# Attention and mixture of experts on one core: GpSimd's row transfers tied to TensorE's results

## The reference, cut to what matters

```python
h = layernorm(x)
q, k_new, v_new = h @ wq.T, h @ wk.T, h @ wv.T
k, v = concat([ctx, k_new]), concat([ctx, v_new])      # 64 cached rows + 64 new ones
x = x + softmax(q @ k.T / 16) @ v @ wo.T
h = layernorm(x)
probs = softmax(h @ router.T)                          # 32 experts
topv, topi = top_k(probs, 4); topv = topv / sum(topv)
out = sum over the 4 of topv * ((silu(h @ w_gate[e]) * (h @ w_up[e])) @ w_down[e])   # inner width 96
out += sigmoid(h @ sgate_w) * ((silu(h @ sw_gate) * (h @ sw_up)) @ sw_down)          # inner width 512
x = x + out
```

## Time and profile before

| what | value |
|---|---|
| median of the timed runs | 516.37 us |
| recorded span of the profiled execution | 667.5 us |
| recorded span less the median | 151.1 us |
| TensorE busy (matmuls, share of the recorded span) | 574.4 us, 86% |
| VectorE busy | 363.5 us, 54% |
| ScalarE busy | 288.7 us, 43% |
| GpSimd busy | 269.4 us, 40% |
| mean granted TensorE clock | 0.903 |

### The profile page before, as it was taken

How to read it: one execution, slowest core, us unless ns; L and a number is a source line. 1 busy time by engine, 2 the same in 40 slices (tenths; PEclk the granted TensorE clock), 3 DMA queues, 4 the chain that set the end, 5 groups by cost and what they waited for, 6 DMA issues and landing times. The chain is left out here.

```text
span 667.5 us, 13365 instructions
## 1 busy us (share of the span) xinstructions
PE 574.4 (86%) x3945; PEld 478.3 (72%) x3945; DVE 363.5 (54%) x1199; ACT 288.7 (43%) x719; POOL 269.4 (40%) x344
## 2 busy tenths in 40 slices
PE   8998787788887777899998988778877898979998
PEld 7997777677777565677886666656666676658886
DVE  5575455555555351565553635445454444536998
ACT  5775444555444440613463545444454544401111
POOL 1004444445555458380034544445454454560000
PEclk9999788987778788699997977988989978989999
DMA  5573544444433322293145444544444544228996
GB/s 160 181 227 128 170 156 129 144 134 145 138 123 113 110 76 107 70 244 98 31 130 148 131 140 124 140 136 139 130 140 140 150 131 132 87 86 330 368 340 230
DMA packets 65956, 100.77 MB, mean 151 GB/s; under 512 B 9856, under 2 KB 52864, under 8 KB 65792
## 3 DMA queue, kind: packets, MB, share of 16 engines
q1 hardware_dynamic: 48704, 60.30, 30.6%
q0 software_dynamic: 12672, 35.41, 14.7%
q10 hardware_dynamic: 4512, 4.23, 1.9%
HBM read 55.92 MB, written 43.97 MB: 150 GB/s over the span
## 5 line engine op out<-in xcount | busy, mean ns | idle before, releaser
L512 POOL DMA_INDIRECT returned<-arena,back x136 | 130.6, 960 | 171.7 <-DVE back L1629 81.5
L481 POOL DMA_INDIRECT sent<-rows,slot x128 | 129.9, 1015 | 159.2 <-issue 82.7
L1100 PE MATMUL bank<-w_gu,arena 128*128 x416 | 94.7, 363 | 26.6 <-issue 16.6
L1100 PEld LDWEIGHTS bank<-w_gu,arena 128*128 128x128 f32 x416 | 73.0, 205 | 32.8 <-issue 32.8
L1580 DVE TENSOR_TENSOR arena<-bank,arena 128x192 f32<-128x192 f32 x68 | 24.2, 356 | 113.5 <-ACT arena L737 94.5
L737 ACT ACTIVATE arena<-bank 128x192 f32<-128x192 f32 x68 | 22.3, 329 | 127.0 <-remote 70.5
L806 PE MATMUL bank<-w_hi_all,att_split 128*128 128x256 f32 x256 | 56.8, 314 | 18.6 <-issue 18.6
L1597 DVE TENSOR_SCALAR arena<-bank,back_to 128x256 f32<-128x256 f32 x136 | 59.0, 476 | 6.3 <-remote 5.3
L806 PE MATMUL bank<-att_split,w_hi_all 128*128 128x256 f32 x256 | 55.5, 336 | 1.4 <-issue 1.3
L710 ACT COPY hnt<-w_gu 128x384 f32 x128 | 55.7, 509 | 0.0
L806 PEld LDWEIGHTS bank<-w_hi_all,att_split 128*128 128x128 f32 x256 | 42.4, 208 | 18.2 <-issue 18.2
(11 more groups left out here) (216 smaller groups left out, 1128.6 us busy)
## 6 DMA issues: line engine op xcount, KB each, us to landing
arena<-returned SPq DMA_DIRECT2D x16, 1024.0 KB, 7.2
loaded<-sent SPq DMA_DIRECT2D x104, 134.0 KB
w_gu<-w_gate_up SPq DMA_DIRECT2D x32, 192.0 KB
sent<-rows SPq DMA_DIRECT2D x4, 1072.0 KB, 6.2
loaded<-sent SPq DMA_DIRECT2D x128, 33.5 KB
resid<-x SPq DMA_DIRECT2D x16, 256.0 KB, 2.9
att_plain<-ctx_t SPq DMA_DIRECT2D x16, 256.0 KB, 3.1
out<-resid ACTq DMA_DIRECT2D x7, 512.0 KB, 4.9
```

Of the source, the lines that this page charges most:

```text
L481: pool.indirect_dma_start(out=sent, out_offset=bass.IndirectOffsetOnAxis(ap=slot[:, 2 * b + j, k:k + 1], axis=0), in_=rows[:, u, j, :], in ...
L512: pool.indirect_dma_start(out=returned, out_offset=bass.IndirectOffsetOnAxis(ap=back[:, t:t + 1], axis=0), in_=down_e[u][:, s, :], in_offs ...
L1100: last = pe.matmul(view[:, s, :], rows_t[:, s, c, :], w_gu[:, c, bass.ds(e[s - 2 + len(e)], 1), :] .rearrange("p e f -> p (e f)"), start=( ...
```

## The change

GpSimd gets two kinds of new waits; nothing else changes. In attention, for 0 < n < 16, each second turn first waits for a result of TensorE's step n: turn 0 for `c_psum` = n, turn 2 for `k_psum` = n+1, turn 4 for `xnt_psum` = n+2, turn 6 for `o_psum` = n. The waits stand only where there is something to send, so from step 5 on. In the experts, the second transfer of pair p waits until the down product of pair p+1 is done.

```diff
                 for turn in range(SENT_A_STEP):
                     if may_send(n - 6 if turn < 4 else n - 5):
+                        if turn % 2 == 0 and 0 < n < blocks:
+                            wait(pool, ("c_psum", "k_psum", "xnt_psum", "o_psum")[turn // 2],
+                                 (n, n + 1, min(n + 2, blocks), n)[turn // 2])
                         send()
                         if n > blocks:
                             breathe(1)
...
                 wait(pool, "down_ready", pair + 1)
                 for s in range(2):
                     t = 2 * pair + s
+                    if s == 1 and pair + 1 < pairs:
+                        wait(pool, "worked_psum", worked(pair + 1))
                     pool.indirect_dma_start(
```

## The result

The changed kernel takes 520.01 us in the median of 20 runs (516.77 to 523.84) against 516.03 for the kernel before; the ratio is 1.0101, 95% interval 1.0074 to 1.0128. It is slower by 1.0%, some 5 us, where no change was forecast. The time lies inside the forecast range, 511.5 to 521, but the direction was missed.

A forecast was written before the change was run, and what follows sets the result against it. TensorE alone was taken as the bound; its unstarved stages sum to 510.9 us, 5.5 below the timed median. The change's terms add 0 to 516.4 us, with +0.9 at worst; forecast 516.4 us, range 511.5 to 521.

The forecast's parts named there:

- The recorded stalls are not in the timed runs: Whole kernel: TensorE's starved stretches belong to the recording; the change can take away at most 5.5 us.
- The sum of unstarved stages: Whole kernel with TensorE never starved: 59.0, 96.0, 101.2, 182.0 and 72.7 us, together 510.9.
- the 151.1 us: Recorded span 667.5 us less timed median 516.4; nearly all of it said to belong to the recording.
- The first transfer 3.7 us later, then each mark already there: Attention: GpSimd's stream starts 3.7 us later; within a step or two the waits are met and cost nothing.
- No wait is added from step 16 on, where steps are longer and GpSimd catches up; so that end doesn't move: After attention's new waits: GpSimd catches up, so SyncE's wait for the last transfer ends as before; cost 0.
- There are over 20 us in any case: Between the end of SyncE's wait for attention transfers and first tile use: over 20 us of slack.
- If the 3.7 us were not absorbed they would be all of it: Attention: the cost is 0, hidden by slack; without that slack, the late start's 3.7 us would be the cost.
- The experts' wait costs nothing: Experts: the 67 added waits are met or nearly met, with slack of 6 us or more; cost 0.
- Rival 2: Experts: GpSimd becomes the bound through restarts after waits, giving 519.5 to 525.8 us; chance 0.13.
- The last landing moves by at most 1.3 us: End of the experts: the last landing doesn't move, at worst by 1.3 us, adding 0.9 us to the time.
- Rival 3: Attention: transfers hold back VectorE's operations, 13 us in all, 529.6 us, chance 0.03; a smaller loss, 518 to 519, 0.05.
- A recorded span of 610 to 665 us: Changed kernel's profile: span expected at 610 to 665 us, against 667.5 before, since waits bind in the recorded execution.

The follow-up runs named there:

- e1: The kernel before the change, unchanged, run and profiled again: 515.74 us, ratio 0.9999.
- e9: The kernel before, with SyncE reading the first four pairs' row numbers ahead of its wait for the attention transfers: 511.86 us, ratio 0.9957.
- e4: The kernel before with a single wait, GpSimd's very first attention transfer waiting for `xnt_psum` of step 5: 518.74 us, ratio 1.0073.
- e6: The kernel before with a single wait, the first attention transfer waiting for the next step's `xnt_psum`: 528.70 us, ratio 1.0304.
- e3: The kernel before with only the new wait in the experts, none in attention: 515.42 us, ratio 0.9989.

## Why the prediction was wrong

- *The recorded stalls are not in the timed runs*: right. The sum of unstarved stages, 510.9 us, met the span of e1, 511.5, and no part of the 151.1 us was there to be won. That the sum met it so well was luck: two terms were off and cancelled. The experts take 191.9 us, not 182.0 (even in e9, where TensorE waits for tile loads for 0.3 us only, the same instructions take 188.8 us, 5.90 a double pair and not 5.69), and the stretch before them 93.7, not 101.2. The text put the stalls down to the recording; e1 was recorded too and has none.
- *The first transfer 3.7 us later, then each mark already there*: right, 3.9 us, and GpSimd slower than TensorE's step, as the row count said.
- *"No wait is added from step 16 on, where steps are longer and GpSimd catches up; so that end doesn't move"*: this is the step that failed. GpSimd had no idle time between 54.2 and 225.2 us in which to catch up, and the end moved, by 1.4 us in the changed kernel and 4.5 in e4. The arithmetic for it stood in the text: 128 transfers at 1.35 us are 173 us, from 56 on, so until 229.
- *"There are over 20 us in any case" between that end and the first tile use*: wrong, and the root of it. The 20 us were read from the execution recorded ahead of the prediction, where TensorE was slowed and GpSimd had gaps of 5 to 10 us. The sum had been moved to the unstarved pace, and this slack had not: by the sum's own terms the first tile use would have come at 59.0 + 96.0 + 101.2 - 11.8 = 244.4 us, with the stream ending at 229. In e1 the last transfer starts at 225.2, the first load goes at 228.8, the first tile is used at 234.7, and about 3 us of lateness are absorbed there (e4, e6). Lateness within these 3 us still costs, behind the first tile, which no term of the prediction had.
- *"If the 3.7 us were not absorbed they would be all of it"*: the price was named, and e4's 3.8 us lie on it, but not by that way: the delay does not pass through one for one. In the changed kernel 1.4 of the 3.9 us reach the loads, and the time grows by 5.2. The case stood beside the rivals rather than as one, with no chance of its own.
- *The experts' wait costs nothing*: right within the noise, e3 at 0.9989. Rival 2 falls. *The last landing moves by at most 1.3 us*: the tail is as long as before, 73.2 against 73.1 us.
- *Rival 3, transfers beside other work of VectorE*: ten attention steps are 95.8 us in both windows, so no such loss is seen. The traces show the hold-up the other way round: the transfer waits for VectorE's operation, and its wait lies inside its recorded time (0.96 to 1.89 us), while the operations of L1296 and L1235 keep theirs whether they start during a transfer or not (684 to 693 and 1218 to 1224 ns in e1). Rows 8 looked at the engine that is not lengthened.
- *A recorded span of 610 to 665 us*: wrong, 516.2, for the reason above.

## What to carry to other kernels

Work out each queue's total (number of instructions times their spacing) and set it against the stretch it has: an engine that shows idle time in one execution can be the bound in another. When a sum is moved to another pace, every slack that it leans on has to be moved too, read from both ends at that pace. A wait put at the head of a stream without idle time is not made good by idle time later, however early it stands, and however quickly the waits behind it cost nothing. What it costs in the end is another question, which only the stage that pays can answer.

## What the runs showed of the hardware

- The timed value and the recorded span of the same execution lie 2.3 us apart (518.55 and 516.2 us; e1: 513.81 and 511.5).
- SyncE needs about 0.5 us to read two row numbers into registers (1.03 against 0.52 us from a pair's last load to the next pair's first, in e1 and e9), as long as from one load to the next within a pair (0.51 to 0.57 us).
- An indirect transfer of GpSimd that starts while a VectorE TENSOR_TENSOR with both inputs in SBUF is running ends 0.83 to 0.84 us after that operation (21 transfers in e1, up to 1.89 us instead of 0.96). Nothing is seen of it where under 0.12 us of the operation are left, nor in two transfers of the changed kernel that start within 0.04 us of the operation's start.
- After 9.8 us without work TensorE's granted clock was 0.53 in the next 7.5 us, and 0.50, the level of 1.2 GHz, in the first 4.1 of them (e6).
